# Audio tower, four layers: two batches taking turns through the first two layers

## What is computed

```python
x: (4, 750, 128)
tok:      relu(context-3 windows @ weight.T + bias)              # -> (4, 748, 128)
L0 attn:  layernorm, gated projections, causal softmax attention, project, residual
L0 ffn:   gate g8 = f(mean over tokens); W1, W2, b1, b2 = base + sum_e g8[e] * task_vector[e]
L1 attn:  rope, attention in a window of 128 keys, @ Wo.T + bo, residual
L1 ffn:   top-2 of 8 experts by token; each expert is a whole transformer block
L2 attn, L2 ffn, L3 attn (8 heads), L3 ffn                       # the "tail"
```

## Time and profile before

| | us |
|---|---|
| median of 3 runs | 4861.89 (4861.24 to 4869.1) |
| profiled execution | 4862.37 |
| its span | 4860.5 |
| PE / PEld busy | 4300.1 / 2396.2 |
| DVE / ACT / POOL busy | 2850.8 / 2933.6 / 688.2 |

### The profile page before, as it was taken

The page is one execution under the profiler, slowest core; times in us unless marked ns, Lnnn a source line. Parts: engine busy times, 40 slices in busy tenths (PEclk is TensorE's granted clock), DMA queues, the critical chain, the costliest instruction groups (busy, mean ns, idle before and its releaser), DMA issues.

```text
span 4860.5 us, 72964 instructions
## 1 busy us (share of the span) xinstructions
PE 4300.1 (88%) x24884; PEld 2396.2 (49%) x24884; DVE 2850.8 (59%) x6683; ACT 2933.6 (60%) x6340; POOL 688.2 (14%) x465
## 2 busy tenths in 40 slices
PE   4666758999999999999999999889889888988988
PEld 3444433444444444444444444345655664565566
DVE  5555457777777777777777777422522442252244
ACT  1211215777787777777787777675466447536644
POOL 0000011222222222222222222100000000000000
PEclk8666668999999999999999999999989999998999
DMA  2000014233342342432433423001010000101000
GB/s 99 14 7 7 13 19 49 42 50 45 46 68 39 48 60 38 60 52 43 53 46 52 58 40 46 19 30 34 1 43 19 16 14 30 34 1 43 22 10 17
DMA packets 102148, 173.47 MB, mean 36 GB/s; under 512 B 19824, under 2 KB 76576, under 8 KB 101408
## 3 DMA queue, kind: packets, MB, share of 16 engines
q1 hardware_dynamic: 101792, 168.99, 20.2%
HBM read 86.73 MB, written 7.92 MB: 19 GB/s over the span
## 4 chain that ended last, share of the span: by engine, by line
issue 47%; PE 47%; DVE 3%; POOL 1%; DVEq 1%; ACT 1%; DMA 0%; SPq 0%; POOLq 0%
PE ps L947 11%; PE ps L983 11%; PE ps L957 10%; PE ps L1017 4%; PE ps L1026 3%; PE ps L938 2%; PE ps L1046 1%; DVE peaks L1719 1%; POOL rstd L645 1%; PE ps L1007 1%; PE ps L754 1%; PE ps L1051 1%; DVE h L1761 1%; DVE gcol L1702 1%; PE ps L966 0%
## 5 line engine op out<-in xcount | busy, mean ns | idle before, releaser
L1719 DVE TENSOR_REDUCE peaks<-ps 128x1 f32<-128x748 f32 (+1 forms) x1536 | 1409.0, 933 | 475.8 <-PE ps L957 453.3
L1347 ACT ACTIVATE masked<-ps 128x384 f32<-128x384 f32 (+3 forms) x1536 | 683.1, 486 | 194.4 <-PE ps L947 182.5
L1347 ACT ACTIVATE probs<-ps 128x384 f32<-128x384 f32 (+1 forms) x1536 | 661.8, 484 | 73.5 <-PE ps L947 73.3
L645 POOL TENSOR_TENSOR rstd<-var,minus_half 128x6 f32<-128x6 f32 x104 | 138.3, 1330 | 3150.6 <-DVE var L1535 3150.6
L947 PE MATMUL ps<-q_stack,k_stack 98*128 98x384 bf16 (+3 forms) x1536 | 450.4, 328 | 1.0
L947 PE MATMUL ps<-shared 98*128 98x384 bf16 (+3 forms) x1536 | 447.2, 327 | 4.4 <-ACT probs L1347 1.7
L957 PE MATMUL ps<-k_stack,q_stack 96*128 96x374 bf16 (+1 forms) x1536 | 381.5, 330 | 38.2 <-DMA k_stack<-parts 25.6
L957 PE MATMUL ps<-shared 96*128 96x374 bf16 (+1 forms) x1536 | 372.1, 323 | 7.6 <-DVE peaks L1719 7.0
L947 PEld LDWEIGHTS ps<-shared 98*128 98x128 bf16 (+1 forms) x1536 | 147.9, 103 | 336.4 <-ACT masked L1347 126.3
L947 PEld LDWEIGHTS ps<-q_stack,k_stack 98*128 98x128 bf16 (+1 forms) x1536 | 149.7, 103 | 329.3 <-ACT masked L1347 121.4
L1277 ACT ACTIVATE probs<-ps,neg_top 128x128 f32<-128x128 f32 (+3 forms) x216 | 131.8, 613 | 245.8 <-DVE neg_top L1598 245.8
(11 more groups left out here) (309 smaller groups left out, 7889.4 us busy)
## 6 DMA issues: line engine op xcount, KB each, us to landing
shared<-parts SPq DMA_DIRECT2D x192, 187.0 KB, 9.1
wr<-in_l SPq DMA_DIRECT2D x32, 580.5 KB, 3.6
q_stack<-parts SPq DMA_DIRECT2D x96, 187.0 KB, 8.0
k_stack<-parts SPq DMA_DIRECT2D x96, 187.0 KB, 10.6
wts<-in_l SPq DMA_DIRECT2D x32, 514.5 KB, 3.6
wrow<-in_l_rows SPq DMA_DIRECT2D x32, 320.0 KB, 4.1
wts<-in_l SPq DMA_DIRECT2D x32, 257.5 KB, 2.6
shared<-in_l SPq DMA_DIRECT2D x4, 2048.0 KB, 9.4
```

The lines of the kernel that those rows point to most:

```text
L645: pool.tensor_tensor(rstd[:, :], var[:, :], minus_half[:, :], ALU.pow).then_inc(S["rstd_ready"], 1)
L1347: act.activation(probs_ring(u)[0:m, 0:hi - lo], src[0:m, 0:hi - lo], ACT.Exp, scale=float(HD) ** -0.5).then_inc(S["ring_done"], 1)
L1719: v.tensor_reduce(peaks[0:m, g, j, head:head + 1], src[0:m, :, 0:T // 2], XY, ALU.max)\
```

## The change

- **Lanes.** The front is written out, no longer a loop. Batches 0 and 1, then 2 and 3, run as lanes 0 and 1. Each engine's front is a generator of seven pieces (0 tok and two norms; 1 L0 attn; 2 gfc1; 3 the small product and both merges; 4 up and down products, three norm-like steps; 5 L1 attn; 6 gates), and `in_turns` issues piece 0 of lane 0, piece 0 of lane 1, piece 1 of lane 0, and so on. Lane 1 has buffers of its own, laid over q_stack0, k_stack0 and parts, and its own `operand_ready`; hid, QT, KT, V, probs, att and PSUM are shared.
- **Engines.** tok's relu goes from DVE to ACT. Both halves of the turned xn, and L1's values, are evicted by ACT. The steps for b1 come ahead of those for W1. Both merges stay on DVE.
- **o1.** Wv and bv of L1 are multiplied by Wo in the setup, so attention adds straight into h; the turned attention and the o1 product go.
- **Gates.** The logits of all batches are kept, and `gating` runs once over 24 tiles. Gates stay on the chip.
- **Hand-over.** POOL sets its constants only after `front_done` of all batches and `lane_free` of the last spill, k_stack0's among them (before, DVE's in the setup). `STAGES` becomes (2, 0, 1, 3).

Cut to its core:

```diff
+LANES = 2
+def in_turns(first, second):
+    for _ in first:
+next(second)
+    assert next(second, None) is None
...
-LAYER1 = Attention(NT, lambda u: 2 * P, float(D) ** -0.5, product_mask="band")
+LAYER1 = Attention(NT, lambda u: 2 * P, float(D) ** -0.5, product_mask="band", summed=True)
...
-STAGES = (B - 1,) + tuple(range(B - 1))
+STAGES = (2, 0, 1, 3)
...
+lanes = (Lane(0, xT=xT[:, :], h=h, xn=xn, x1=x1, y=y, xnT=xnT[:, :], merged=merged[:, :],
...
+         Lane(1, xT=parts_room[:, 0:X_END], h=tokens(q_room[:, TPAD:TPAD + TP]),
+              xn=tokens(q_room[:, TPAD + TP:TPAD + 2 * TP]), x1=tokens(k_room[:, 0:TP]),
+              y=tokens(k_room[:, TP:2 * TP]), xnT=k_room[:, 2 * TP:2 * TP + TPAD],
...
+lg_all = by_token(KT[:, 1, 0:W_LG])
+v_room = V[:, :, :].rearrange("p t d -> p (t d)")
+lg2_all, ex_all, pick_all, cand_all = (by_token(v_room[:, i * W_LG:(i + 1) * W_LG]) for i in range(4))
...
-    def spill(b, following=None):
...
-        sp.dma_start(saved["h"][b, :, :], flat(h)).then_inc(S["h_spilled"], 16)
-        if following is not None:
-            load_x(following)
-        sp.wait_ge(S["front_done"], n.take("front_done"))
-        sp.dma_start(saved["xn"][b, :, :], flat(xn)).then_inc(S["front_spilled"], 16)
-        sp.dma_start(saved["xT"][b, :, :], xT_).then_inc(S["front_spilled"], 16)
-        sp.dma_start(saved["gates"][b, :, :], flat(gates)).then_inc(S["front_spilled"], 16)
-        sp.wait_ge(S["h_spilled"], n.take("h_spilled", 16))
-        sp.sem_inc(S["h_free"], 1)
-        sp.wait_ge(S["front_spilled"], n.take("front_spilled", 48))
-        sp.sem_inc(S["front_free"], 1)
+        sp.dma_start(lane.xT[:, 0:T_IN], A["xT"][b, :, :]).then_inc(S[f"x_loaded{lane.k}"], 16)
+    def spill(first):
+        for b in range(first, first + LANES):
+            sp.wait_ge(S["h_ready"], n.take("h_ready"))
+            sp.dma_start(saved["h"][b, :, :], flat(lanes[b % LANES].h)).then_inc(S["h_spilled"], 16)
+            if b + LANES < B:
+                load_x(b + LANES)
+        for b in range(first, first + LANES):
+            sp.wait_ge(S["front_done"], n.take("front_done"))
+            sp.dma_start(saved["xn"][b, :, :], flat(lanes[b % LANES].xn)).then_inc(S["front_spilled"], 16)
+            sp.dma_start(saved["xT"][b, :, :], lanes[b % LANES].xT_).then_inc(S["front_spilled"], 16)
+        sp.wait_ge(S["h_spilled"], n.take("h_spilled", 16 * LANES))
+        sp.wait_ge(S["front_spilled"], n.take("front_spilled", 32 * LANES))
+        sp.sem_inc(S["lane_free"], LANES)
     def spill_merged(b):
...
         pool.drain().then_inc(S[done], 1)
     def experts():
+        pool.wait_ge(S["front_done"], n.take("front_done", B))
+        pool.wait_ge(S["lane_free"], n.take("lane_free", LANES + B))
         pool.memset(lift[:, T:TP], 0.0)
...
         pool.memset(k_stack1[STACK:STACK + SHIFT, :, :], -1.0)
+        pool.drain()
+        pool.memset(k_stack0[STACK:STACK + SHIFT, :, :], -1.0)
         pool.drain().then_inc(S["shared_ready"], 1)
         split()
...
+            power(norms, lane)
+            yield
+    for b in range(0, B, LANES):
+        in_turns(front(lanes[0]), front(lanes[1]))
     experts()
     with n.loop(pool, "tail", B, S["loop_entered"]):
...
+    pe.transpose(ps[:, 0, P:2 * P], C("k2"), ident)
+    pe.transpose(ps[:, 0, 2 * P:3 * P], C("v1"), ident)
...
     pe.matmul(ps[:, 1, P:2 * P], probs[:, 0, P:2 * P], C("hk2"), start=True, stop=True)
-    pe.matmul(ps[:, 1, 2 * P:3 * P], probs[:, 0, 0:P], probs[:, 0, P:2 * P], start=True, stop=True)\
+    pe.matmul(ps[:, 1, 2 * P:3 * P], probs[:, 0, 0:P], probs[:, 0, P:2 * P], start=True, stop=True)
+    pe.matmul(ps[:, 1, 3 * P:4 * P], probs[:, 0, 2 * P:3 * P], C("o1"), start=True, stop=True)
+    pe.matmul(ps[0:1, 2, 0:P], probs[:, 0, 3 * P:3 * P + 1], C("o1"), start=True, stop=True)\
         .then_inc(S["fold_ready"], 1)
...
+            [(lane.xT[:, t * P + i:(t + 1) * P + i], tw[:, i * P:(i + 1) * P]) for i in range(CONTEXT)],
+            "tok_done_a")
+        yield
+        turn_x(lane)
         feat([C("expand_q"), C("expand_k"), C("expand_lin"), C("expand_pre")], xT_, False)
...
-        pe.wait_ge(S["operand_ready"], n.take("operand_ready"))
+        operand()
...
-        turn(att)
+        operand()
+        turn(att, True)
...
-        turn(xn)
+        yield
+        turn_x(lane)
         feat([C("gfc1")], xT_)
-        pe.wait_ge(S["operand_ready"], n.take("operand_ready"))
-        pe.matmul(ps[:, 4, 0:8], spread[:, :], C("gfc2"), start=True, stop=True).then_inc(S["tok_ready"], 1)
-        pe.wait_ge(S["operand_ready"], n.take("operand_ready"))
-        feat([merged[:, f * P:(f + 1) * P] for f in range(FT)], xT_)
-        pe.wait_ge(S["operand_ready"], n.take("operand_ready"))
-        tok(NT, lambda t: [(tile_of(hid[:, f, :], t), merged[:, F + f * P:F + (f + 1) * P]) for f in range(FT)],
-            "tok_done_v")
-        turn(xn)
+        yield
+        operand()
+        pe.matmul(ps[:, 4, 0:8], lane.spread[:, :], C("gfc2"), start=True, stop=True)\
+            .then_inc(S["tok_ready"], 1)
+        pe.wait_ge(S["tok_done_v"], n.take("tok_done_v"))
+        yield
+        operand()
+        feat([lane.merged[:, f * P:(f + 1) * P] for f in range(FT)], xT_)
+        operand()
+        tok(NT, lambda t: [(tile_of(hid[:, f, :], t), lane.merged[:, F + f * P:F + (f + 1) * P])
+                           for f in range(FT)], "tok_done_v")
+        yield
...
+        tok(NT + 1, lambda t: [(vrow[:, t * P:(t + 1) * P], row(R("bv1"))), (tile_of(lane.xnT, t), C("v1"))],
+            "tok_done_a")
         pe.wait_ge(S["feat_done"], n.now("feat_done"))
-        pe.wait_ge(S["operand_ready"], n.take("operand_ready"))
+        operand()
         attention(LAYER1, lambda u: tile_of(QT[:, 0, :], u), lambda u: keyT[:, u * P:(u + 2) * P],
                   lambda u, j: V[:, u + j, :], D)
-        turn(att)
-        tok(NT, lambda t: [(tile_of(attT, t), C("o1"))], "tok_done_v")
-        turn(xn)
+        operand()
+        yield
+        turn_x(lane)
         feat([C("gate_k")], xT_)
         tok(NT, lambda t: [(tile_of(hid[:, 0, :], t), C("queries"))], "tok_done_v", 8)
+        yield
...
-    with n.loop(act, "front", B, S["loop_entered"]):
-        n.take("tok_ready", NT)
-        turned(xT_)
+    def front(lane):
+        act.wait_ge(S["lane_free"], n.take("lane_free"))
+        for t in range(NT):
+            act.wait_ge(S["tok_ready"], n.take("tok_ready"))
+            act.activation(lane.h[:, t, :], ps[:, 4 + t % 4, 0:D], ACT.Relu).then_inc(S["tok_done_a"], 1)
...
-        n.take("tok_ready", NT + 1)
+        values(V, NT + 1)
         attention(LAYER1)
-        turned(attT)
-        n.take("tok_ready", NT)
-        turned(xT_)
+        yield
...
-        gate_exponentials(NT)
+        yield
+    for b in range(0, B, LANES):
+        in_turns(front(lanes[0]), front(lanes[1]))
+    gate_exponentials(B * NT, ex_all, lg2_all)
     experts()
     with n.loop(act, "tail", B, S["loop_entered"]):
...
-    for buf in (xT, xnT, attT, add_w):
+    for buf in (xT, xnT, attT, add_w, keyT, lanes[1].xT, lanes[1].xnT):
         v.memset(buf[:, :], 0.0)
...
-    v.memset(k_stack0[STACK:STACK + SHIFT, :, :], -1.0)
...
-    v.tensor_copy(probs[:, 0, 0:2 * P], ps[:, 0, 0:2 * P]).then_inc(S["fold_done"], 1)
...
+    v.tensor_copy(C("v1"), ps[:, 1, 3 * P:4 * P])
+    v.tensor_copy(row(R("bv1")), ps[0:1, 2, 0:P])
...
-        v.wait_ge(S["h_free"], n.take("h_free"))
-        tok_measured(lambda t, product: v.tensor_scalar(h[:, t, :], product[:, 0:D], 0.0, None, ALU.max), h)
-        v.drain().then_inc(S["x_free"], 1)
-        norm(h, x1, True)
-        v.wait_ge(S["front_free"], n.take("front_free"))
-        norm(x1, xn)
+    def front(lane, b):
...
+        for t in range(NT):
+            v.wait_ge(S["tok_done_a"], n.take("tok_done_a"))
+            v.bn_stats(lane.stats[:, t, :], h[:, t, :])
+        n.take("tok_ready", NT)
+        norm(h, x1, True, lane)
+        norm(x1, xn, False, lane)
         ready()
-        turned(xT_)
+        yield
...
-        tok_measured(add_to_h, h)
-        norm(h, xn, True)
+        tok_measured(lambda t, product: v.tensor_tensor(h[:, t, :], product[:, 0:D], h[:, t, :], ALU.add), h,
+                     lane)
+        norm(h, xn, True, lane)
         ready()
-        turned(xT_)
+        yield
...
+        yield
         v.wait_ge(S["tok_ready"], n.take("tok_ready"))
-        v.tensor_tensor(g8[:, :], ps[:, 4, 0:8], R("gfc2_b"), ALU.add)
+        v.tensor_tensor(g8[:, :], ps[:, 4, 0:8], R("gfc2_b"), ALU.add).then_inc(S["tok_done_v"], 1)
         v.drain()
+        for e in range(E):
+            v.scalar_tensor_tensor(lane.merged_b1, C("tv_b1")[:, e * FT:(e + 1) * FT], g8[:, e:e + 1],
+                                   C("b1") if e == 0 else lane.merged_b1, ALU.mult, ALU.add)
+            v.drain()
         v.wait_ge(S["tasks_loaded"], 16)
```

(65 more changed lines are left out.)

195 lines of the change are left out of this document (129 added, 66 removed).

## The result

The kernel after takes 4728.05 us (median of 4 runs, 4722.52 to 4733.03), beside 4862.46 us for the one before: ratio 0.9721, 95% interval 0.9703 to 0.9738. The forecast was 4720, with 4685 to 4768 as range. The profiled execution took 4722.52 us; that is the one to set against the sum of the steps. The four executions of this kernel took 4722.5, 4723.1, 4733.0 and 4733.0 us, so its median is only good to about 5 us. Where a difference to this kernel is small, the traces are set beside the medians, by the start of the first expert product (571.84 us here) or of the first peak (600.32).

What follows compares the result with a forecast made beforehand. A chain passing between engines, none full, was taken to bound the front. 39.3 + 2.2 + 2 x 254 + 17.5 = 567 us against 709.0, 142 less, gives 4720 us; range 4685 to 4768.

Steps and rivals of the forecast that it cites:

- The likeliest case: Whole kernel: the forecast itself, two interleaved pairs of 254 us in the front, 4720 us; chance 0.52.
- The gain is the overlap: Front: a second batch fits in the gaps of the first's chain, a pair taking 254 us against 334.5.
- Case C: Front: turns but no overlap, four lanes in line taking 642 us, total 4855; chance 0.03.
- The merge bounds the pair's middle: Piece 3: merges hold DVE 20 us a lane; TensorE idles 20 us until DVE's g8 of lane B.
- The pair's length: Front: both lanes laid out piece by piece, 265 us at present clock levels, 254 with 11 taken off.
- The clock term: B1, A2, B2, B5, A6, B6: upper clock level kept without gaps, up to 14 us a pair, 11 taken.
- case B: Front: less overlap, clock levels as now (+22) or some 1 us per piece for hand-overs, 4742 to 4768; chance 0.22.
- tok at 1.2 GHz: Start of each lane: all of tok stays at the lower level, 2.30 us a tile, 27.6 us a pair.
- case A: tok: runs at the upper level, about 1.1 us a tile, -14 to -27 us, 4690; chance 0.2.
- Edges: Setup and hand-over: the o1 fold adds 2.2 us ahead of tok, POOL's late memsets 17.5 ahead of the experts.
- Keys to stacks to first peak keeps its length: Start of the experts: the way from the first key product to the first peak was forecast unchanged.
- Rival D, fetched code: Written-out front: 4.00 us of code fetch at each of 28 pieces on DVE and TensorE, 224 us, 4944; chance 0.03.

Runs made afterwards that it cites:

- run 1: Kernel after with the two lanes of each pair run one after the other instead of in turns: 4852.6 us.
- run 2: Kernel before with the o1 fold alone (Wv and bv of L1 multiplied by Wo in the setup): 4851.91 us.
- runs 3 to 5: Kernel after with both lanes' small product ahead of any merge, 4726.96 us; four DVE steps a lane added in the merge piece, 4740.64, or gates' piece, 4723.13.
- run 11: Kernel after with tok's bias product contracting over 128 rows (zeros added) instead of one: 4699.14 us.
- Run 7: Kernel after with TensorE waiting for POOL's constants only ahead of the first scores, and POOL's first split ahead of its memsets: 4713.04 us.
- run 10: Kernel after without the start wait ahead of the experts, plus dense bf16 products in TensorE's waits in setup and gates' pieces: 4689.38 us.
- run 8: Kernel after with fourteen dense bf16 products, results unused, ahead of lane A's tok in each pair: 4714.97 us.
- runs 11 and 12: The second of these: kernel after without the start wait, with dense products in waits, first-layer scores and tok's bias over 128 rows: 4658.49 us.

## Why the prediction was right, and where it was off

The likeliest case happened: 4728 against 4720, nearer to it than to any rival's time; against the profiled execution, from which the sum was made, it is 4722.5 against 4720.4. The mechanism is right; part of the nearness is misses that cancel, as the end of this section shows. By its own steps:

- **The gain is the overlap.** Shown by run 1 (124.5 us) and run 2 (the fold 9.6, the rest nothing on balance). Case C fell as a description of the change, but its sum of 642 us for lanes in line was right: 642.1.
- **The merge bounds the pair's middle.** One idle stretch of about 20 us that ends with g8: 19.65 and 19.79. DVE's piece of 20 us: 20.04. That the merges are the bound, and not TensorE's wait, is what runs 3 to 5 show.
- **The pair's length: 254 forecast, 258.6 and 256.6 measured.** The clock term of this sum was over-sized. With the level kept in every stretch, the working gives 204.6 - 5.1 = 199.5 us from tok's start to A5's scores and 60.2 - 9.3 = 50.9 behind them; 11 of these 14 us were taken. Measured are 202.6 and 56.0 in the first pair: 3.1 more ahead and 5.1 more behind. Of the 3.1, 1.2 stand there at lane A's first scores, and 1.0 is lane B's piece 4 on DVE, for which the working gave 14.9 us where it gave lane A 16.3 (182.9 to 197.8), and which took 15.9. Of the 5.1, 3.2 are lane B's gates' piece: its 3.0 us of clock were not granted. Its products are as long as before the change, while lane A's feature product was 1.52 us:

```profile
290.99 1.54 PE L808 MATMUL ps<-const,q_stack 128*128 128x128 f32 x6 [0.26 <-DVE KT L2049]
293.09 2.86 PE L822 MATMUL ps<-k_stack,const 128*128 128x384 f32 x4 [0.56 <-ACT k_stack L1347]
```

  In between stand lane A's queries of 8 columns. Another 1.3 are the two attentions, which begin at the lower level: the granted clock is 0.54 in 240 to 250, and B5's scores, at 270.27, begin with 1.22 us for one group of 256 columns, as at the lower level in the earlier trace rows, not the 0.64 of later ones. The rest is tenths in each piece, as case B has them for hand-overs; no run separates them.
- **tok at 1.2 GHz: right.** Within each lane all tiles lie 2.30 us apart, 24 in all, and in the second pair the granted clock is 0.50 with TensorE busy 9.63 and 10.00 of 10:

```profile
305.00:315.00 10.00, 9.63 (x34) 7.77 (x35) 1.86 (x11) 1.11 (x4) 0.00 (x0) 0.50 0.01 2
315.00:325.00 10.00, 10.00 (x38) 8.20 (x37) 6.17 (x29) 1.11 (x4) 2.64 (x2) 0.50 0.00 1
```

  So case A did not happen. The Trainium skill (TensorE: Matmul & The Clock Gate, "Part 1: The HAM clock gate (the 'warmup' mystery)") ties the level to how busy the engine is. This trace disagrees for these products, busy 10.00 of 10 us at 0.50; run 11 shows that the one-row bias among them is what keeps the level down.
- **Edges.** tok starts 1.7 us later, forecast 2.2. The hand-over costs 15.6 and not 17.5, as spill and semaphores took 3.7 and not 5.5 (the forecast's terms as written add up to 17.1). One sentence was wrong: "Keys to stacks to first peak keeps its length". It went from 32.3 us (709.00 to 741.33 in the trace before) to 28.5 (571.84 to 600.32). Before, SP issued the first stacks 10.2 us after the keys' product: the last batch's spill, which stands ahead of them, was issued only at 715.52, behind the gating of that batch. Now they are issued 6.45 us after it. Run 7 shows that these 3.8 us are not a gift of the start wait: without that wait the length is 28.6. That the gating behind the spill is the cause is read from the order of the trace, not tried. From the first peak to the end it is 4119.2 before and 4120.4 after, nothing, as forecast.
- **Rival D, fetched code.** Not seen: a lane in written-out code takes 159.4 to 162.3 us in run 1, against 163.8 for a turn of the loop with the same fold (run 2), where the rival had 5 us and more for each of its pieces.

The misses add up: 2 x 254 became 515.2 (+7.2), the hand-over gave 1.9, tok's start 0.5, together 4.8: 571.8 instead of 567. Behind it, 3.8 came back and 1.2 was lost, which leaves 2 us. That is luck: the pairs alone were 7.2 off.

## What to carry to other kernels

Two independent chains that each leave every engine half idle are worth interleaving: lay both out on each engine's fixed order with one chain's own durations, and look for the piece where one engine is needed twice running; its length is the gap that remains. Here work added to that engine there was paid in full, and moving the other engine's wait gained nothing; taking work off it was not tried. Before believing a level of TensorE's clock to be given, look at how many rows its products contract over: padding 16 rows and one row with zeros to 128 adds no columns, and gained 26 and 29 us by the medians (22 and 21 in the traces), each about a fifth of the 134 us of the whole rewrite.

## What the hardware showed that was not expected

- **Few rows, low clock.** With scores over 16 rows TensorE is granted 0.50 to 0.52 while busy 9.64 and 9.78 of 10 us; over 128 rows, 1.00 while busy 4.38 of 5. With a one-row product among four of tok, the level doesn't rise in two lanes of tok, and can be lost in it while busy 10.00 of 10 (run 10), though it was kept once in both pairs (run 8); with 128 rows it rises by itself in the third or fourth tile (run 11) and is kept through tok (runs 11 and 12). How the chip weighs rows was not measured, only these two counts against 128. Nor do the runs tell few rows from the change between few and 128 rows: padding removes both.
- **A one-row product among full ones costs time of its own.** Tiles of tok with the one-row bias take 0.60 us more at the lower level and 0.39 more at the upper, for the same columns. The Trainium skill (TensorEngine Tiling (Array Packing), "Key Properties") says that changing the tiling mode drains TensorE; the trace agrees with that sign, though no run here separates a drain from another cost of the one-row product.
- **Still open.** The second layer's values also alternate a one-row bias with full products, and the level is lost in their midst in the kernel after, with no gap ahead of it (timeline):

```profile
234.77 0.49 PE L867 MATMUL ps<-const,xnT 128*128 128x128 f32 x2
235.19 0.48 PE L867 MATMUL ps<-rows,const 1*128 1x128 f32 x2
235.60 0.80 PE L867 MATMUL ps<-const,xnT 128*128 128x128 f32 x2
```

  The forecast had no clock term for lane A's values, which lie under DVE's rope; what the loss costs was not measured. The same cure suggests itself. It was not tried.
